# One attention and expert layer: projections moved ahead of the attention steps, the end reordered, and the first residual and normalisation handed to TensorE, GpSimd and ScalarE

## The chip, the cores and the metric

The program runs on one core of one Trainium2 chip. The metric is the device time of one execution in microseconds; the kernel before took 244.71 us (median of 3 runs, 243.72 to 245.84).

## What the reference computes

```python
x = L0_attn_x                                    # (8, 256, 128), 8 batches, 2048 tokens
Q, K, V = x @ Wq + bq, x @ Wk + bk, x @ Wv + bv  # 16 heads of 8
attended = softmax(Q K^T / sqrt(8)) V            # 256 x 256 scores per head and batch
x = layernorm(x + attended @ Wo + bo)            # no gain, no offset
shared = (silu(x @ sw1) * (x @ sw3)) @ sw2       # 256 hidden
s = sigmoid(x @ router_w.T)                      # 8 experts; the top two of s + router_bias are picked
gates = s_sel / (sum of the two s_sel + 1e-9)
routed = sum over experts e of gates_e * (gelu(x @ ew1[e]) @ ew2[e])   # 128 hidden each
x = layernorm(x + shared + routed)
```

All in float32.

## The kernel before

Tokens lie in 8 batches of 256 and, for the feed-forward part, in 4 groups of 512. The whole order is written by hand in `lay_out_slots` (L65 to L142): a list of slots, each with at most one maxima step `m`, one scores step `s`, steps of probabilities times V `pv`, and a list of jobs. Every engine walks the same list and does its part of each slot, in order; semaphores alone hold the engines together.

- The first 14 slots are the **prologue**: the first projections of batch 0, maxima steps 0 to 11, and jobs that project later tokens: `k`, `q`, `v` with a unit number (512 tokens each).
- The **attention slots** s = 0 to 63 follow, 8 per batch. In each, TensorE forms scores for two heads (L819, into the two `ring` banks) and, 12 steps ahead, the maxima products (L828, three `max_bank`s); VectorE reduces the maxima (L656); ScalarE takes the exponent (L554); TensorE multiplies by V (L845). A scores product reuses the ring bank of the slot before, so it waits for that slot's exponent.
- Jobs of the batch just finished sit in the next batch's slots: `norm` (slot 2 of 8), `attT` (3), `wo` (4: the product with Wo, then residual add L695 and statistics L699, L702 on VectorE), `y` (5: GpSimd makes 1/sqrt of the variance, L480, L481, and writes the normalised rows, L483), `yT` (slot 8, which is slot 0 of the batch after: transposed, ScalarE writes the high part L610, VectorE the low part L706), `router` (9). The float32 products with the feed-forward weights use such high and low parts (three passes, L799 to L801). `route...`, `rank`, `den` are the top-two selection, on GpSimd and VectorE; `combT` and `load gates` send the gates through DRAM so that they can be read back to all partitions.
- `shift` (slot 4) splits the maxima and sends them through ScalarE's DMA queue (L605) to the query stack.
- The **end** has 40 units: for each, TensorE forms the upward product (`unit`), ScalarE the nonlinearity (L627 tanh for shared units, L629 Gelu for experts), VectorE the gated product (L761, L764 or L769), and two slots later TensorE accumulates the downward product (`down`, L981). Units 0 to 7 are the shared ones, 8 to 39 the experts of groups 0 to 3. Inside the first units lie the jobs of batch 7; the last group's selection is on VectorE (L720 to L753). Each group ends with `accT`, `finT`, `rstd2`, `norm2` and a store.

## Time and profile before

| | |
|---|---|
| median of 3 runs | 244.71 us |
| profiled execution, its own time | 239.34 us |
| its span, first to last instruction | 237.5 us |
| mean granted TensorE clock | 0.955 of full speed |
| TensorE, VectorE, ScalarE, GpSimd busy | 211.6, 159.9, 135.9, 98.7 us |

The profiled execution is 5.4 us under the median. Times in views count from the first instruction of the span. A granted clock of 1.00 is 2.4 GHz and 0.50 is 1.2 GHz. A share of busy time mixes stages, so each stage is read in its own stretch.

### The profile page before, as it was taken

The page shows a single profiled execution, that of the slowest core. Times are in us where ns is not written, and L with a number is a line of the kernel's source. Part 1 is how long each engine was busy: PE and PEld are TensorE (multiplying, and loading weights), DVE is VectorE, ACT ScalarE, POOL GpSimd, SP SyncE. Part 2 cuts the span into 40 slices and gives each one's busy share as a digit, 9 for nine tenths or more (in the row PEclk, how much of TensorE's full clock was granted, in tenths as well). Part 3 has the DMA queues.
Part 4 walks back from the last instruction along what each step waited for, and adds up shares of the span by engine and source line. Part 5 has one row for each costly group of instructions (what it writes and reads, how often), then busy time and mean ns, then how long its engine had stood idle before and what let it go on. Part 6 is the DMA issues. An engine that isn't in the chain of part 4 may idle for free.

```text
span 237.5 us, 4492 instructions
## 1 busy us (share of the span) xinstructions
PE 211.6 (89%) x1538; PEld 120.8 (51%) x1538; DVE 159.9 (67%) x354; ACT 135.9 (57%) x278; POOL 98.7 (42%) x187
## 2 busy tenths in 40 slices
PE   7997999889899989999899999986788999999970
PEld 7754754354445555546454555653434555555530
DVE  6689686479579899989993223663594365565644
ACT  2996266678777878777778874221524333434330
POOL 8888950244247669573956084042000002020203
PEclk9998559999979999999999999999999999999996
DMA  5471770243134100018000630000000260731011
GB/s 164 133 203 44 187 287 10 59 105 97 46 88 107 49 6 4 8 30 330 6 3 7 217 142 0 3 0 4 0 0 3 91 266 0 265 132 44 3 34 55
DMA packets 10422, 19.19 MB, mean 81 GB/s; under 512 B 1952, under 2 KB 7008, under 8 KB 9760
## 3 DMA queue, kind: packets, MB, share of 16 engines
q1 hardware_dynamic: 8976, 17.06, 22.4%
q10 hardware_dynamic: 1040, 1.05, 1.3%
q0 software_dynamic: 384, 0.79, 1.2%
q8 instruction: 13, 0.21, 0.4%
q14 instruction: 9, 0.07, 0.1%
HBM read 12.80 MB, written 1.11 MB: 59 GB/s over the span
## 4 chain that ended last, share of the span: by engine, by line
PE 64%; DVE 17%; ACT 9%; issue 5%; POOL 2%; ACTq 1%; POOLq 0%; DVEq 0%
PE ring L819 14%; PE pv_bank L845 11%; PE max_bank L981 8%; DVE top L656 4%; ACT probs_mem L554 4%; PE max_bank L828 3%; PE sum_bank L981 3%; PE ring L799 3%; PE ring L801 3%; PE ring L800 3%; DVE hid L769 2%; PE pv_bank L853 2%; DVE stats L780 2%; PE sum_bank L900 2%; PE misc_bank L900 1%
## 5 line engine op out<-in xcount | busy, mean ns | idle before, releaser
L656 DVE TENSOR_REDUCE top<-max_bank 128x2 f32<-128x512 f32 x128 | 80.9, 681 | 12.8 <-PE max_bank L828 12.7
L554 ACT ACTIVATE probs_mem<-ring 128x512 f32<-128x512 f32 x128 | 70.2, 597 | 20.3 <-PE ring L819 18.7
L819 PE MATMUL ring<-qstack,kstack 32*128 32x256 f32 x256 | 46.0, 338 | 6.4 <-ACT probs_mem L554 4.2
L828 PE MATMUL max_bank<-kstack,qstack 32*128 32x256 f32 x256 | 45.7, 349 | 1.2 <-DVE top L656 0.9
L819 PEld LDWEIGHTS ring<-qstack,kstack 32*128 32x128 f32 x256 | 29.5, 192 | 26.5 <-ACT probs_mem L554 14.5
L845 PE MATMUL pv_bank<-probs_mem,v 128*18 128x256 f32 x512 | 41.4, 396 | 0.4 <-ACT probs_mem L554 0.4
L629 ACT ACTIVATE xt<-ring 128x512 f32<-128x512 f32 x32 | 19.1, 597 | 35.2 <-PE ring L801 35.2
L769 DVE TENSOR_TENSOR hid<-xt,gates_mem 128x512 f32<-128x512 f32 x32 | 21.9, 689 | 22.3 <-ACT xt L629 22.2
L981 PE MATMUL max_bank<-hid,wf 128*128 128x512 f32 x60 | 31.8, 612 | 2.1 <-DVE hid L769 1.5
L828 PEld LDWEIGHTS max_bank<-kstack,qstack 32*128 32x128 f32 x256 | 29.1, 198 | 6.0 <-DVE top L656 1.9
L799 PE MATMUL ring<-yt_hi,wf_lo 128*128 128x512 f32 x40 | 30.7, 767 | 0.0
L489 POOL TENSOR_SCALAR rstd<-mv 128x4 f32<-128x4 f32 (+1 forms) x5 | 2.2, 441 | 65.1 <-DVE mv L783 65.0
L470 POOL TENSOR_TENSOR gates_mem<-gates_mem 128x512 fp32r<-128x512 f32 x6 | 7.6, 1268 | 20.9 <-ACT gates_mem L595 20.9
L801 PE MATMUL ring<-yt_hi,wf_hi 128*128 128x512 f32 x40 | 15.8, 395 | 0.0
L800 PE MATMUL ring<-yt_lo,wf_hi 128*128 128x512 f32 x40 | 15.8, 395 | 0.0
L845 PEld LDWEIGHTS pv_bank<-probs_mem,v 128*18 128x18 f32 x512 | 8.7, 97 | 9.9 <-issue 1.0
L981 PEld LDWEIGHTS max_bank<-hid,wf 128*128 128x128 f32 x60 | 9.6, 188 | 8.0 <-DVE hid L769 6.2
L627 ACT ACTIVATE xt<-ring 128x512 f32<-128x512 f32 x8 | 4.8, 597 | 14.8 <-PE misc_bank L801 7.0
L483 POOL TENSOR_SCALAR xs<-res,mv,rstd 128x128 f32<-128x128 f32 x16 | 12.7, 801 | 0.9
L799 PEld LDWEIGHTS ring<-yt_hi,wf_lo 128*128 128x128 f32 x40 | 7.6, 190 | 9.3 <-issue 7.9
L800 PEld LDWEIGHTS ring<-yt_lo,wf_hi 128*128 128x128 f32 x40 | 7.6, 190 | 8.6 <-issue 8.6
L981 PE MATMUL sum_bank<-hid,wf 128*128 128x512 f32 x20 | 10.7, 619 | 1.3 <-DVE hid L769 1.1
(211 smaller groups left out, 320.8 us busy)
## 6 DMA issues: line engine op xcount, KB each, us to landing
gates_mem<-gate_scratch SPq DMA_DIRECT2D x4, 2048.0 KB, 7.7
kstack<-gates_mem SPq DMA_DIRECT2D x36, 64.0 KB, 2.1
qstack<-gates_mem SPq DMA_DIRECT2D x24, 64.0 KB, 2.1
wf<-w_ffn_dram SPq DMA_DIRECT2D x1, 1408.0 KB, 7.4
xs<-x_dram SPq DMA_DIRECT2D x4, 256.0 KB, 5.6
xt<-x_t_dram SPq DMA_DIRECT2D x3, 256.0 KB, 4.3
qstack<-gates_mem POOLq DMA_DIRECT2D x12, 64.0 KB, 2.6
out_dram<-xs SPq DMA_DIRECT2D x3, 256.0 KB, 2.3
```

The lines of the kernel that those rows point to most:

```text
L483: ins = pool.tensor_scalar(xs[:, QT * n + t, :], res1[:, t, :], mv1[:, t, 0:1], rstd1[:, t:t + 1], ALU.subtract, ALU.mult)
L554: nc.scalar.activation(probs[:, i % 2, s_heads(s)[r], :], ring_of(("scores", 2 * s + r))[:, :], ACT.Exp, scale=SCALE).then_inc(probs_made, 1)
L629: nc.scalar.activation(act_out[:, b % 2, :], bank[:, :], ACT.Gelu).then_inc(act_made, 1)
L656: dve.tensor_reduce(top[:, m_heads(m)[r], t, :], max_bank[(2 * m + r) % NMAX][:, :].rearrange("p (h k) -> p h k", h=2), AX.X, ALU.max).the ...
L769: dve.tensor_tensor(hid[:, b % NHB, :], act_out[:, b % 2, :], gates_mem[:, g % 2, e * GT:(e + 1) * GT], ALU.mult).then_inc(hid_dve, 1)
L799: mm(out_ap, w_lo, m_hi, start=first, stop=False)
L800: mm(out_ap, w_hi, m_lo, start=False, stop=False)
L801: return mm(out_ap, w_hi, m_hi, start=False, stop=last)
L819: ins = mm(ring_of(("scores", 2 * s + r))[:, kt * S:(kt + 1) * S], kstack[rows, t, k:k + P], qstack[rows, t, b * S:(b + 1) * S], start=Tru ...
L828: ins = mm(max_bank[(2 * m + r) % NMAX][:, qt * S:(qt + 1) * S], qstack[rows, t, q:q + P], kstack[rows, t, b * S:(b + 1) * S], start=True, ...
L845: ins = mm(pv_bank[32 * j:32 * j + 2 * VW, 0:S], v[:, (QT * b + kt) * H // 2 + HPS * n + j, k * VW:(k + 2) * VW], probs[:, p // 2 % 2, j, ...
L981: mm(acc_bank[g][:, :], wf[:, c:c + P], hid[:, b % NHB, :], start=n == 0, stop=n == NSH + NE - 1).then_inc(down_made, 1)
```

## The change

It has three parts.

1. Prologue: units 1 and 0 of V are projected earlier and units 2 of K and Q move from attention slots 6 and 8 into the prologue; unit 1 of V uses a ring bank. K, Q and V of unit 3 move from slots 16 to 21 to slots 8 to 13, V of unit 2 from slot 11 to 4. The stores of unit 2 stand in slot 0, ahead of the load of the feed-forward weights on SyncE.
2. End: the first eight units are the experts of group 0, the next eight the shared ones, then the experts of groups 1 to 3. The jobs of batch 7 stand further apart (`norm` 2, `attT` 4, `wo` and `y` 5, `yT` 10, `router` 12), `router` of batch 6 moves into the end, and the last group's selection runs on GpSimd and VectorE like that of the others. Before, each batch's `router` was one slot after `yT`; now three slots after. `hid` now shares the memory of `probs`.
3. First residual: TensorE adds x by a product with the identity (new L924), VectorE's statistics read PSUM, GpSimd makes 1/sqrt and the shift, ScalarE writes the normalised rows (new L636). ScalarE copies the transposed rows (new L642) and GpSimd makes both parts (new L508, L509).

```diff
@@ -69,8 +71,8 @@
         slots[n + 2].m = n
     for n, job in ((0, ("first", 0)), (0, ("first", 1)), (0, ("high", 0)), (1, ("first", 2)),
                    (2, ("first", 3)), (2, ("first", 4)), (3, ("first", 5)), (4, ("first", 6)), (5, ("first", 7)), (7, ("k", 1)),
-                   (8, ("store", (1, 1))), (9, ("q", 1)), (9, ("store", (1, 0))), (10, ("shift", 0)), (12, ("v", 0)),
-                   (12, ("split rw", 0))):
+                   (8, ("v", 1)), (8, ("store", (1, 1))), (9, ("q", 1)), (9, ("store", (1, 0))), (10, ("shift", 0)),
+                   (10, ("v", 0)), (11, ("k", 2)), (12, ("split rw", 0)), (13, ("q", 2))):
         slots[n].jobs.append(job)
     at, m = {}, 12
...
-    put(0, ("load w", 0))
+    put(0, ("store", (2, 1)), ("store", (2, 0)), ("load w", 0))
     put(1, ("bo", 0))
-    put(2, ("add bo", 0))
-    put(3, ("v", 1))
-    put(4, ("add bo", 1))
-    for s, unit in ((6, 2), (16, 3)):
-        put(s, ("k", unit))
-        put(s + 1, ("store", (unit, 1)))
-        put(s + 2, ("q", unit))
-        put(s + 4, ("store", (unit, 0)))
-        put(s + 5, ("v", unit))
-        put(s + 6, ("add bo", unit))
+    for n in range(NG):
+        put(2 + 2 * n, ("add bo", n))
+    put(4, ("v", 2))
+    for n, job in ((8, ("k", 3)), (9, ("store", (3, 1))), (10, ("q", 3)), (12, ("store", (3, 0))), (13, ("v", 3))):
+        put(n, job)
     for n in range(PIECES):
         put(18 + 2 * n, ("split w", n))
     for b in range(1, NB):
         slot = next(n for n in range(len(slots)) if slots[n].m == 8 * b + 7) + 1
         slots[slot].jobs.insert(0, ("shift", b))
+    route = (("route0", 1), ("sig", 2), ("route1", 3), ("route2", 4), ("route3", 6), ("rank", 8), ("route4", 9), ("den", 10),
+             ("route5", 11))
     for b in range(NB - 1):
         first = 8 * (b + 1)
-        for kind, n in (("norm", 2), ("attT", 3), ("wo", 4), ("y", 5), ("yT", 8), ("router", 9)):
+        for kind, n in (("norm", 2), ("attT", 3), ("wo", 4), ("y", 5), ("yT", 8)):
             put(first + n, (kind, b))
+        if b < NB - 2:
+            put(first + 11, ("router", b))
         if b % 2:
-            g = b // 2
-            for kind, n in (("route0", 10), ("sig", 11), ("route1", 12), ("route2", 13), ("route3", 15), ("rank", 17),
-                            ("route4", 18), ("den", 19), ("route5", 20)):
-                put(first + n, (kind, g))
-            put(first + 22, ("combT", b - 1))
-            put(first + 23, ("combT", b))
-            if g < 2:
-                put(first + 25, ("load gates", g))
-
-    unit_at = [NHALF + u + (u >= 6) for u in range(NUNITS)]
-    for u, s in enumerate(unit_at):
-        put(s, ("unit", u))
-        put(s + 2, ("down", u))
-    for kind, n in (("norm", 1), ("attT", 2), ("wo", 3), ("y", 3), ("yT", 6), ("router", 7), ("route a", 8), ("route b", 9),
-                    ("route c", 10)):
-        put(NHALF + n, (kind, NB // 2 - 1 if kind.startswith("route ") else NB - 1))
-    put(NHALF + 12, ("combT", NB - 2))
-    put(NHALF + 13, ("combT", NB - 1))
+            for kind, n in route:
+                put(first + 11 + n, (kind, b // 2))
+            if b // 2 < 2:
+                put(first + 24, ("combT", b - 1))
+                put(first + 25, ("combT", b))
+                put(first + 27, ("load gates", b // 2))
+    for u in range(NUNITS):
+        put(NHALF + u, ("unit", u))
+        put(NHALF + u + 2, ("down", u))
+    for n, job in ((2, ("norm", NB - 1)), (4, ("attT", NB - 1)), (5, ("wo", NB - 1)), (5, ("y", NB - 1)), (8, ("router", NB - 2)),
+                   (9, ("combT", 4)), (10, ("yT", NB - 1)), (10, ("combT", 5)), (12, ("router", NB - 1)), (12, ("load gates", 2)),
+                   (24, ("combT", NB - 2)), (25, ("combT", NB - 1)), (26, ("load gates", 3))):
+        put(NHALF + n, job)
+    for kind, n in route:
+        put(NHALF + 12 + n, (kind, NG - 1))
     for g in range(NG):
-        s = unit_at[NSHARED + NE * g + NE - 1]
-        if g < 2:
-            put(s + 2, ("load gates", g + 2))
+        s = NHALF + last_of(g)
...
+        latest, rotation = {}, 0
+
+        early_bank = {("v", 1): (ring[1], 6), ("v", 0): (pv_bank, 7)}
         for n, slot in enumerate(slots):
-            banks = [misc_bank, sum_bank] if n < tail else [misc_bank] + max_bank[1:] if n < tail + 3 else [misc_bank, pv_bank]
+            banks = ([misc_bank, sum_bank] if n < tail else [misc_bank, max_bank[2]] if n < tail + 3
+                     else [misc_bank, pv_bank, max_bank[2]] if n < tail + 14 else [misc_bank, pv_bank])
             for kind, u in slot.jobs:
...
                     if kind == "y":
                         pool.wait_ge(stats_made, n + 1)
                         chain(pool.tensor_scalar(rstd1[:, :], mv1[:, :, 1], EPS, None, ALU.add))
+                        pool.tensor_scalar(shift1[:, :], mv1[:, :, 0], -1.0, None, ALU.mult)
                         chain(pool.tensor_tensor(rstd1[:, :], rstd1[:, :], minus_half[:, 0:QT], ALU.pow))
-                        for t in range(QT):
-                            ins = pool.tensor_scalar(xs[:, QT * n + t, :], res1[:, t, :], mv1[:, t, 0:1],
-                                                     rstd1[:, t:t + 1], ALU.subtract, ALU.mult)
-                        ins.then_inc(y_made, 1)
+                        pool.tensor_tensor(shift1[:, :], shift1[:, :], rstd1[:, :], ALU.mult).then_inc(rstd_made, 1)
+                    if kind == "yT":
+                        wait_taken(pool, (kind, n))
+                        c = slice(n * S, (n + 1) * S)
+                        chain(pool.tensor_scalar(yt_hi[:, c], yt_raw[:, n % 2, :], 1.0, None, ALU.mult))
+                        pool.tensor_tensor(yt_lo[:, c], yt_raw[:, n % 2, :], yt_hi[:, c].bitcast(F32), ALU.subtract).then_inc(yt_made, 1)
...
                     if kind == "attT":
                         nc.scalar.copy(att_t[:, :], misc[:, 0:S]).then_inc(misc_act, 1)
+                    if kind == "y":
+                        act.wait_ge(rstd_made, b + 1)
+                        for t in range(QT):
+                            ins = nc.scalar.activation(xs[:, QT * b + t, :], misc_of(("wo", b))[:, t * P:(t + 1) * P], ACT.Identity,
+                                                       bias=shift1[:, t:t + 1], scale=rstd1[:, t:t + 1])
+                        ins.then_inc(y_made, 1)
                     if kind == "yT":
-                        nc.scalar.copy(yt_hi[:, b * S:(b + 1) * S], misc[:, 0:S]).then_inc(yt_hi_made, 1)
+                        if b >= 2:
+                            act.wait_ge(yt_made, b - 1)
+                        nc.scalar.copy(yt_raw[:, b % 2, :], misc[:, 0:S]).then_inc(misc_act, 1)
...
                     if kind == "wo":
                         dve.wait_ge(misc_made, made[kind, b])
-                        dve.wait_ge(xb_made, b // 2 + 1)
                         if b:
                             dve.wait_ge(y_made, b)
-                        dve.tensor_tensor(res1[:, :, :], misc[:, 0:S].rearrange("p (t d) -> p t d", t=QT),
-                                          xs[:, QT * b:QT * b + QT, :], ALU.add).then_inc(misc_dve, 1)
-                        wait_taken(dve, (kind, b))
                         for t in range(QT):
-                            ins = dve.bn_stats(stats1[:, t, :], res1[:, t, :])
+                            ins = dve.bn_stats(stats1[:, t, :], misc[:, t * P:(t + 1) * P])
                         chain(ins)
...
                     if kind == "wo":
                         wait_taken(pe, ("attT", b))
+                        pe.wait_ge(xb_made, b // 2 + 1)
                         for t in range(QT):
-                            ins = mm(misc[:, t * P:(t + 1) * P], att_t[:, t * P:(t + 1) * P], wa[:, 3, :],
-                                     start=True, stop=True)
+                            mm(misc[:, t * P:(t + 1) * P], att_t[:, t * P:(t + 1) * P], wa[:, 3, :], start=True, stop=False)
+                            ins = mm(misc[:, t * P:(t + 1) * P], ident[:, :], xs[:, QT * b + t, :], start=False, stop=True)
                         ins.then_inc(misc_made, 1)
```

How instructions move. First, TensorE in the prologue, from the first `k` job to the first scores product (L900 and new L892: Q or K projection; L903 and new L895: V projection, except that the new L903 is the shift's transpose, which was L911). Before:

```order
L900 MATMUL misc_bank<-xt,wa 128x512
L828 MATMUL max_bank<-kstack,qstack 128x256 x8
L900 MATMUL sum_bank<-xt,wa 128x512
L828 MATMUL max_bank<-kstack,qstack 128x256 x4
L911 MATMUL misc_bank<-ident,top_parts 32x128 x2
L828 MATMUL max_bank<-kstack,qstack 128x256 x8
L903 MATMUL sum_bank<-wa,xt 128x128 x4
L828 MATMUL max_bank<-kstack,qstack 128x256 x4
L819 MATMUL ring<-qstack,kstack 128x256
```

Now:

```order
L892 MATMUL misc_bank<-xt,wa 128x512
L819 MATMUL max_bank<-kstack,qstack 128x256 x4
L895 MATMUL ring<-wa,xt 128x128 x4
L819 MATMUL max_bank<-kstack,qstack 128x256 x4
L892 MATMUL sum_bank<-xt,wa 128x512
L819 MATMUL max_bank<-kstack,qstack 128x256 x4
L903 MATMUL misc_bank<-ident,top_parts 32x128 x2
L895 MATMUL pv_bank<-wa,xt 128x128 x4
L819 MATMUL max_bank<-kstack,qstack 128x256 x4
L892 MATMUL sum_bank<-xt,wa 128x512
L819 MATMUL max_bank<-kstack,qstack 128x256 x8
L892 MATMUL misc_bank<-xt,wa 128x512
```

Three projections stand there that were not: V of unit 1, K of unit 2 and, last before the scores, Q of unit 2.

Second, ScalarE from slot 3 to slot 8 of a batch in the middle (`probs_mem` is the exponent, `xs` the normalised rows). Before:

```order
L608 COPY att_t<-misc_bank 128x256
L554 ACTIVATE probs_mem<-ring 128x512 x2
L602 CAST top_rows<-sum_bank 32x256
L605 DMA qstack<-top_rows 8x4x256
L554 ACTIVATE probs_mem<-ring 128x512 x2
L562 COPY att_raw<-pv_bank 128x256
L554 ACTIVATE probs_mem<-ring 128x512 x6
L610 CAST yt_hi<-sum_bank 128x256
```

Now:

```order
L632 COPY att_t<-misc_bank 128x256
L578 ACTIVATE probs_mem<-ring 128x512 x2
L626 CAST top_rows<-sum_bank 32x256
L629 DMA qstack<-top_rows 8x4x256
L578 ACTIVATE probs_mem<-ring 128x512 x2
L586 COPY att_raw<-pv_bank 128x256
L636 ACTIVATE xs<-misc_bank,shift,rstd 128x128 x2
L578 ACTIVATE probs_mem<-ring 128x512 x6
L642 COPY yt_raw<-sum_bank 128x256
```

The two new activations stand between the exponents of slot 5 and those of slot 6, and wait for GpSimd.

Third, ScalarE at the start of the end (L661 Gelu, L659 tanh, L646 the router's exponent). Before there was one table load, at unit 8:

```order
L614 ACTIVATE expl<-pv_bank 128x16
L627 ACTIVATE xt<-ring 128x512
L629 ACT_TABLE_LOAD
L629 ACTIVATE xt<-ring 128x512 x4
L620 COPY comb_t<-pv_bank 8x256
```

Now:

```order
L661 ACT_TABLE_LOAD
L661 ACTIVATE xt<-ring 128x512
L586 COPY att_raw<-pv_bank 128x256
L661 ACTIVATE xt<-ring 128x512 x4
L632 COPY att_t<-max_bank 128x256
L661 ACTIVATE xt<-ring 128x512
L636 ACTIVATE xs<-misc_bank,shift,rstd 128x128 x2
L661 ACTIVATE xt<-ring 128x512 x2
L659 ACTIVATE xt<-ring 128x512
L646 ACT_TABLE_LOAD
L646 ACTIVATE expl<-max_bank 128x16
L659 ACTIVATE xt<-ring 128x512
```

A third load follows at unit 16. The normalised rows of batch 7 stand between the Gelus of units 5 and 6.

## Rows read from the trace of the kernel before

**Rows 1.** Busy time by stretch: span, PE, PEld, DVE, ACT, POOL (count), clock, DMA.
```profile
84.00:126.00 42.00, 39.67 (x460) 22.02 (x454) 38.95 (x90) 32.98 (x71) 28.61 (x69) 1.00 0.14 55
```

**Rows 2.** Same view for the exponents (L554): busy, count, clock, by batch, half batch.
```profile
28.30:44.65 16.35, 8.91 (x16) 0.79 0.39 130
44.65:59.50 14.85, 8.72 (x16) 1.00 0.40 100
59.50:77.05 17.55, 8.70 (x16) 0.90 0.32 81
77.05:90.25 13.20, 8.81 (x16) 1.00 0.10 26
...
28.30:36.90 8.60, 4.56 (x8) 0.59 0.69 232
36.90:44.65 7.75, 4.36 (x8) 1.00 0.06 16
```

**Rows 3.** Busy time of one microsecond of the prologue, columns as in rows 1.
```profile
21.00:22.00 1.00, 0.26 (x4) 0.06 (x2) 0.93 (x3) 1.00 (x2) 0.79 (x1) 0.82 0.44 113
```

**Rows 4.** Timeline of the prologue: start, length, engine, line, [idle before, its releaser].
```profile
19.70 1.13 PE L900 MATMUL sum_bank<-xt,wa 128*128 128x512 f32 x2
25.01 2.08 PE L903 MATMUL sum_bank<-wa,xt 128*128 128x128 f32 x8
28.33 0.60 ACT L554 ACTIVATE probs_mem<-ring 128x512 f32<-128x512 f32 x1 [0.60 <-PE ring L819]
```

**Rows 5.** Timeline of ScalarE around K of unit 2 in attention slot 6.
```profile
40.22 1.10 ACT L554 ACTIVATE probs_mem<-ring 128x512 f32<-128x512 f32 x2
42.27 0.69 ACT L591 ACTIVATE gates_mem<-sum_bank,wa 128x512 fp32r<-128x512 f32 x1 [0.95 <-PE sum_bank L900]
43.42 1.08 ACT L554 ACTIVATE probs_mem<-ring 128x512 f32<-128x512 f32 x2
```

**Rows 6.** Timeline around one batch's Wo product, by engine.
```profile
111.91 0.61 PE L930 MATMUL misc_bank<-wa,att_t 128*128 128x128 f32 x4
115.79 0.38 PE L819 MATMUL ring<-qstack,kstack 32*128 32x256 f32 x1
...
112.86 0.41 DVE L695 TENSOR_TENSOR res<-misc_bank,xs 128x256 f32<-128x256 f32 x1
113.83 0.25 DVE L702 BATCH_NORM_AGGREGATE mv<-stats 128x2 f32<-128x6 f32 x2
...
115.11 0.22 POOL L480 TENSOR_SCALAR rstd<-mv 128x2 f32<-128x2 f32 x1
116.25 1.59 POOL L483 TENSOR_SCALAR xs<-res,mv,rstd 128x128 f32<-128x128 f32 x2
...
114.44 0.61 ACT L554 ACTIVATE probs_mem<-ring 128x512 f32<-128x512 f32 x1
```

**Rows 7.** One source line, ns of one: activations with bias and scale from memory.
```profile
L582 ACT ACTIVATE probs_mem<-ring,first_cols x8: 556/568/587, 6.4 to 15.2; 128x256 fp32r<-128x256 f32 x8
```

**Rows 8.** Timeline of the end: last exponents, table load, downward products and a stall.
```profile
142.44 1.08 ACT L554 ACTIVATE probs_mem<-ring 128x512 f32<-128x512 f32 x2 [0.38 <-PE ring L819]
...
170.22 1.28 ACT L629 ACT_TABLE_LOAD   x1
...
154.68 1.02 PE L981 MATMUL max_bank<-hid,wf 128*128 128x512 f32 x2
...
157.34 1.02 PE L981 MATMUL max_bank<-hid,wf 128*128 128x512 f32 x2
...
162.42 0.38 PE L952 MATMUL pv_bank<-ident,comb 128*8 128x128 f32 x2 [2.67 <-POOL comb L530]
...
228.94 1.12 PE L981 MATMUL max_bank<-hid,wf 128*128 128x512 f32 x2 [0.44 <-DVE hid L769]
```

**Rows 9.** The chain that ended last: downward products, eight units apart.
```profile
210.37 1.12 PE max_bank L981 x2
...
224.13 1.12 PE max_bank L981 x2
```

More of the change, by code:

```diff
@@ L38 @@
 NSHARED = NG * NSH
+SHARED = range(NE, NE + NSHARED)
 NUNITS = NG * (NSH + NE)
@@ L146, in group_of, with first_of, last_of @@
 def group_of(u):
-    return divmod(u, NSH) if u < NSHARED else ((u - NSHARED) // NE, NSH + (u - NSHARED) % NE)
+    if u in SHARED:
+        return divmod(u - SHARED.start, NSH)
+    e = u if u < NE else u - NSHARED
+    return e // NE, NSH + e % NE
+def first_of(g):
+    return min(u for u in range(NUNITS) if group_of(u)[0] == g)
+def last_of(g):
+    return max(u for u in range(NUNITS) if group_of(u)[0] == g)
 FIN = [(g, 0, TPG) for g in range(NG - 1)] + [(NG - 1, t, t + TPG // 2) for t in (0, TPG // 2)]
@@ L325, in wait_taken @@
                 wait_hid(eng, u[1])
+            elif taker(u) == "y":
+                eng.wait_ge(y_made, u[1] + 1)
             else:
@@ L329, in wait_bank @@
         def wait_bank(eng, u):
-            if before[u] is not None:
+            if u in early_bank:
+                eng.wait_ge(first_read, early_bank[u][1])
+            elif before[u] is not None:
                 wait_taken(eng, before[u])
@@ L563, in _ @@
                 for kind, b in slot.jobs:
-                    if TAKER.get(kind) == "act" or kind == "yT":
+                    if TAKER.get(kind) == "act":
                         act.wait_ge(misc_made, made[kind, b])
@@ L730, in _ @@
-                    if kind == "route b":
-                        chain(dve.tensor_scalar(tie[:, :, :, :], diff[:, :, :, :], 0.0, None, ALU.is_equal))
-                        chain(dve.tensor_scalar(diff[:, :, :, :], diff[:, :, :, :], 0.0, None, ALU.is_gt))
-                        for t in range(TPG):
-                            ins = dve.tensor_tensor(tie[:, t, :, :], tie[:, t, :, :], earlier[:, :, :], ALU.mult)
-                        chain(ins)
-                        chain(dve.tensor_tensor(diff[:, :, :, :], diff[:, :, :, :], tie[:, :, :, :], ALU.add))
-                        dve.tensor_reduce(rank[:, :, :], diff[:, :, :, :], AX.X, ALU.add).then_inc(route_dve, 1)
@@ L809, in wait_ring @@
                     pe.wait_ge(probs_made, n + 1)
-                elif n < NSHARED:
-                    pe.wait_ge(sh_read, n + 1)
+                elif n in SHARED:
+                    pe.wait_ge(sh_read, n - SHARED.start + 1)
                 else:
```

80 lines of the change are left out of this document (27 added, 53 removed).

## The prediction

> **What bounds the kernel now.** I read the stages first, because no engine is the limit throughout. In the middle of attention two engines are nearly full: of 42 us TensorE is busy 39.67 and VectorE 38.95, ScalarE 32.98 [rows 1]. The exponents mark the batches: 13.20 us for an undisturbed one, 16.35 for the first and 17.55 for the third [rows 2]. The first is long because the granted clock is 0.50 (1.2 GHz) for most of its first half: 8.60 us against 7.75 for the second half, although that one carries a K projection [rows 2]. The clock fell in the microsecond in which TensorE had only 0.26 us of work [rows 3]. A K or Q projection inside attention lengthens its slot to 43.42 - 40.22 = 3.20 us, since ScalarE takes its two copies before the next exponents [rows 5]; the next slot, up to 44.65 [rows 2], takes 1.23, so one costs 1.95. The third batch has two of them. The end lasts from the last exponent, 143.52, to the last downward product, 230.06: 86.5 us [rows 8]. In its dense part eight units take 13.76 us [rows 9]; its first part has stalls, the longest 2.67 us, where TensorE waits for GpSimd's gates [rows 8].
>
> **A, the prologue.** V of unit 1, K and Q of unit 2 are added ahead of the first scores. At full clock each is 1.1 us of TensorE (1.13 for a Q projection) [rows 4], 3.3 in all. The first fills the hole in which the clock fell, and V of unit 0, 2.08 us at half clock [rows 4], should then take half. I expect the clock to hold and the extra work to be nearly absorbed; but Q of unit 2 stands last, and its two copies by ScalarE (0.69 each [rows 5]) come before the first exponent. That one moves from 28.33 to about 29.4: +1.1. First batch: two halves like the second, without its K: 2 x (7.75 - 1.95) = 11.6, plus 0.6 for V of unit 2 and 0.4 for the Wo bias, an estimate: 12.6, rounded up to 12.8 since its jobs differ, against 16.35: -3.5. Second: loses one projection, gains two: +1.95. Third: becomes like the fourth, 13.20 for 17.55: -4.35. Sum **A = -4.8**. If the clock falls as before, the two added projections cost 2.1 us each, the first exponent comes 4.6 later, the first batch gains 2.4 instead of 3.5 and A is -0.2. On SyncE the 24 stores of unit 2 now precede the weight load. They are due at maxima step 32, in attention slot 20, and the weights in slot 18, both over 20 us later; I cost them at nothing, and were they late, TensorE's maxima of slot 20 would wait.
>
> **B, the first residual.** VectorE loses the add of 0.41 [rows 6] and the low part, about as long since it too reads 256 columns of PSUM. TensorE gains two products of the kind of the Wo ones, whose four records take 0.61 with their overlap [rows 6]; I take 0.45 for the two. GpSimd trades two 0.8 us operations [rows 6] for three or four small ones and the two parts, which nothing needs for three slots. Statistics read from PSUM have no row; from no change up to 0.2 more each, since the add that reads twice the columns from there takes 0.41. I take no change, because reading PSUM has not made that add slow.
> What decides is the new wait on ScalarE. Take the batch of [rows 6]. The aggregate ends at 114.08; without the add at 113.65. GpSimd takes 1.14 from L480 to L483, and two more small operations of 0.22 with gaps add 0.5: 115.4, if GpSimd is free. ScalarE then writes two tiles: an activation with both operands from memory is 0.57 us for 256 columns [rows 7], so 0.45 to 0.57 for 128; I take 0.9 for both: 116.3. Only then comes the exponent of slot 6, 0.61: 116.9 instead of 115.05. The scores of slot 7 reuse its bank and started at 115.79 [rows 6]; they start 1.1 later. Behind them wait the maxima and VectorE. About 0.3 comes back, since VectorE has caught up by then and the router's product fills a wait three slots later: **0.8 per batch** for five batches, 4.0. For batch 0 V of unit 3 lies in the same slot and covers the wait: 0.1. Batch 7's slots have no maxima to hide behind: 0.45 for the product and 0.85 for the wait, together 1.3. **B = +5.4.** Bounds per batch: -0.4 (the add's time passes through, the wait is covered) and +1.9.
>
> **C, the end.** Walked with the prices of the rows, from the last exponent: first downward product after transposing, 1.28 for the table load [rows 8], 0.60 Gelu and 0.69 product: 4.0. Six more experts with three jobs of batch 7: 11.3. Then unit 6's Gelu waits behind the same chain as in B, and its downward product is 2.1 late. Eight shared units, 157.34 - 154.68 = 2.66 each less a wait of 0.28 there [rows 8], with two router products, four transposes and a finish among them: 22.4. Remaining 24 units at 1.62 with two finishes and the last steps: 42.9 (13.76 for eight with a finish [rows 9]). Sum 82.7 against 86.5: **C = -3.9** with rounding. The 2.67 stall and VectorE's selection between the first experts are gone. The second table load has about 2 us of cover from TensorE's work on unit 9, the third about as much as it takes.
> Each load is 1.28 us here, followed at once by its activation [rows 8]. The Trainium skill (ScalarE: Activation LUTs, What ACT_TABLE_LOAD costs) gives 2.66 us for a switch with a drain, and its section on table sets asks to group activations by set. That speaks against two more loads. The trace shows no drain.
>
> **Sum.** -4.8 + 5.4 - 3.9 = -3.3 on 239.34: 236.0 for a profiled execution. That execution is 5.4 under the median of the runs; the difference applied to 244.71 gives **241.4**. What a measurement can tell from no change is 1%, 2.4 us: under 242.3 is faster, over 247.2 slower.
>
> **The rivals.**
> - Forecast, 0.43: 241.4, own range 238.5 to 245. For it: every step stands in a queue order.
> - The clock falls in the prologue all the same, 0.20. VectorE's reductions pace the prologue, so TensorE keeps holes. A = -0.2, total +1.3: 246.0.
> - VectorE's relief passes through and the wait on ScalarE is covered, 0.17. For it: VectorE is busy 38.95 of 42 us [rows 1] and loses 0.8 per batch. Against: the exponent of slot 6 is behind the wait. B = 7 x -0.4 = -2.8, total -11.5: 233.2.
> - Slower, 0.12: GpSimd is late. In the shown batch the aggregate was ready at 114.08 and L480 began at 115.11, because the selection's operations were ahead of it in GpSimd's queue [rows 6]. Now ScalarE, and behind it TensorE, would wait for that. It decides from 1.6 us per batch on; at +1.0 more for seven batches the total is -3.3 + 7.0 = +3.7: 248.4. Against: the selection now starts a slot after `y`.
> - Switches cost more than their load, 0.08. A drain of half a load to a whole one behind the first and the third would sit on the path: at 1.3 each nearly +2.5, 243.9. The Trainium skill's 2.66 us (ScalarE: Activation LUTs, What ACT_TABLE_LOAD costs) is this rival's size.
>
> The first and last are on the faster or the same side by their spread (0.43 gives 0.27 faster, 0.15 same), the second same or slower. **Faster 0.50, same 0.31, slower 0.19.** Range 233.5 to 248.5: from just above the third case's value, half of which lies below, to the fourth's; it leaves out about 0.1 below and 0.08 above.
>
> **What would show it.** Clock: no 0.50 before the first exponent, which starts near 29.4; batches of 12.7, 16.8 and 13.5 us. B: ScalarE idle before L636 until GpSimd's L504, 0.7 us or more in most batches; batch periods in the middle 0.8 above 13.3, and VectorE well under its 93%. C: 82 to 84 us from last exponent to last downward product, first one about 4 us in, a stall of about 2 us at unit 6. The prediction fails if the clock drops in another place, if the ScalarE wait is under 0.3 us, or if GpSimd starts L501 late.

## The result, and the profile after

The changed kernel takes 254.94 us (median of 6 runs, 251.58 to 262.17), the kernel before 244.42 beside it (240.35 to 246.08): ratio 1.0427, 95% interval 1.0236 to 1.0618. 241.4 was forecast, with 233.5 to 248.5 as the range. It is slower by 4.3%. The ratio leaves out runs more than 1.5% above the fastest of their kernel (it compares 251.58, 252.26 and 253.26 with 240.35 and 243.72), and since single runs of one kernel lie up to 5.5% apart, the main differences below are given on the medians and between the fastest runs.

The profiled execution took 251.58 us, its span is 249.8, against 239.34 and 237.5. Its page:

```profile
span 249.8 us, 4579 instructions
PE 222.4 (89%) x1570; PEld 127.5 (51%) x1570; DVE 153.5 (61%) x317; ACT 143.6 (58%) x296; POOL 110.7 (44%) x224
PEclk9999956999995699979999798699999999999997
```

The third line is the granted clock in 40 slices. Before, it had one deep dip, at 22 to 35 us, and a shallow one. Now there are five: 5 and 6 from 31 us on, 5 and 6 from 75 on, 7 at 106, 7 at 137, and 8 and 6 from 150 on (a slice is 6.2 us). The batches, as in [rows 2] by the exponents' line (span, busy ScalarE, clock):

```profile
30.15:45.60 15.45, 8.80 (x16) 0.67 0.48 130
45.60:62.70 17.10, 8.68 (x16) 1.00 0.54 168
62.70:78.25 15.55, 8.80 (x16) 0.91 0.08 22
78.25:95.20 16.95, 8.68 (x16) 0.78 0.01 3
95.20:109.75 14.55, 8.69 (x16) 0.99 0.01 3
109.75:125.70 15.95, 8.66 (x16) 0.90 0.35 136
125.70:140.30 14.60, 8.69 (x17) 1.00 0.01 3
140.30:156.00 15.70, 8.68 (x16) 0.83 0.35 136
```

Every batch from the fourth on is longer than the 13.20 of [rows 2]. The two at the full clock take 14.55 and 14.60; the others, where the clock fell, 15.7 to 16.95. Three engines are less busy than in [rows 1], although the stretch is longer (44 us for 42):

```profile
95.20:139.20 44.00, 40.15 (x436) 22.06 (x436) 32.45 (x73) 32.78 (x73) 27.44 (x71) 0.96 0.13 52
```

VectorE fell from 38.95 of 42 us to 32.45 of 44, so its relief came, and bought nothing. The timeline around one batch's normalisation shows where the time sits. The columns are those of [rows 6]:

```profile
134.96 1.08 ACT L578 ACTIVATE probs_mem<-ring 128x512 f32<-128x512 f32 x2 [0.91 <-PE ring L810]
135.00 0.25 DVE L730 BATCH_NORM_AGGREGATE mv<-stats 128x2 f32<-128x6 f32 x2
135.34 0.24 POOL L501 TENSOR_SCALAR rstd<-mv 128x2 f32<-128x2 f32 x1 [1.65 <-DVE mv L730]
136.66 0.19 POOL L504 TENSOR_TENSOR shift<-shift,rstd 128x2 f32<-128x2 f32 x1
136.89 0.81 ACT L636 ACTIVATE xs<-misc_bank,shift,rstd 128x128 f32<-128x128 f32 x2 [0.58 <-POOL shift L504]
137.59 1.08 ACT L578 ACTIVATE probs_mem<-ring 128x512 f32<-128x512 f32 x2
138.23 0.98 PE L810 MATMUL ring<-qstack,kstack 32*128 32x256 f32 x4 [1.08 <-ACT probs_mem L578]
138.83 1.08 ACT L578 ACTIVATE probs_mem<-ring 128x512 f32<-128x512 f32 x2 [0.16 <-PE ring L810]
```

ScalarE waits 0.58 us for GpSimd's last small operation (L504), writes the rows (0.81), and only then comes the exponent of slot 6, at 137.59. Behind it TensorE stood still for 1.08 us. Such a hole, 1.05 to 1.08 long, lies in six batches: it ends at 75.20, 93.15, 107.69, 123.68, 138.23 and 153.94. The clock in the stretches after some of them, and after the longest hole of all, which lies behind the first exponents:

```profile
28.90:30.80 1.90, 0.53 (x9) 0.31 (x8) 1.55 (x3) 1.78 (x4) 1.90 (x5) 1.00 0.75 219
31.00:32.00 1.00, 1.00 (x8) 0.62 (x8) 0.53 (x1) 0.82 (x2) 0.98 (x3) 0.55 0.72 207
75.00:86.00 11.00, 10.80 (x86) 4.93 (x86) 6.58 (x11) 6.30 (x14) 3.69 (x8) 0.53 0.01 1
109.00:113.00 4.00, 4.00 (x40) 1.99 (x36) 2.02 (x4) 2.35 (x6) 1.35 (x4) 0.57 0.01 2
140.00:144.00 4.00, 4.00 (x29) 1.69 (x28) 0.00 (x0) 2.58 (x6) 1.01 (x2) 0.57 0.02 6
154.00:161.00 7.00, 7.00 (x36) 3.56 (x37) 0.70 (x1) 4.08 (x7) 4.34 (x7) 0.51 0.00 1
```

The clock is 0.50 (1.2 GHz) from just after the holes that end at 30.80 and 75.20, from about 2 us after those of 107.69 and 138.23, and from at once after that of 153.94. After those of 93.15 and 123.68 it stayed at 1.00. A hole is thus no certain fall, but every fall up to here follows one (e1 and e11 will show falls that follow none). The two profiled executions, before and after, laid side by side:

| | forecast | measured |
|---|---|---|
| first exponent, 28.33 to 30.18 | +1.1 | +1.85 |
| batches 0 to 2, 48.76 to 48.10 | -5.0 | -0.66 |
| batches 3 to 6, 53.82 to 62.02 | +3.2 | +8.20 |
| batch 7, 12.61 to 15.61 | +1.3 | +3.00 |
| last exponent to last downward product, 86.54 to 86.38 | -3.9 | -0.16 |
| sum | -3.3 | +12.2 |

The forecast column is A, B and C put where they act. Only the second batch came out as forecast (17.10 for 16.8 + 0.1).

### The profile page after: what moved, and what is told of

Read it like the earlier page. It is cut to its first block and busy times, and to the rows that moved or that the text cites. A ratio compares the mean times of both kernels' runs of the same rounds, so it can differ in the third digit from the quotient of the medians.

```text
span 249.8 us, 4579 instructions
## 1 busy us (share of the span) xinstructions
PE 222.4 (89%) x1570; PEld 127.5 (51%) x1570; DVE 153.5 (61%) x317; ACT 143.6 (58%) x296; POOL 110.7 (44%) x224
## 3 DMA queue, kind: packets, MB, share of 16 engines
q10 hardware_dynamic: 1040, 1.05, 1.3%
## 5 line engine op out<-in xcount | busy, mean ns | idle before, releaser
L810 PE MATMUL ring<-qstack,kstack 32*128 32x256 f32 x256 | 49.2, 360 | 10.9 <-ACT probs_mem L578 9.3
L810 PEld LDWEIGHTS ring<-qstack,kstack 32*128 32x128 f32 x256 | 31.1, 206 | 37.5 <-ACT probs_mem L578 26.9
L819 PE MATMUL max_bank<-kstack,qstack 32*128 32x256 f32 x256 | 47.0, 355 | 1.1 <-DVE top L688 0.8
L836 PE MATMUL pv_bank<-probs_mem,v 128*18 128x256 f32 x512 | 45.7, 436 | 0.0
L760 DVE TENSOR_TENSOR probs_mem<-xt,gates_mem 128x512 f32<-128x512 f32 x32 | 22.4, 703 | 34.7 <-ACT xt L661 34.7
L661 ACT ACTIVATE xt<-ring 128x512 f32<-128x512 f32 x32 | 19.0, 597 | 30.3 <-PE ring L792 29.3
L971 PE MATMUL max_bank<-probs_mem,wf 128*128 128x512 f32 x60 | 32.0, 614 | 1.8 <-DVE probs_mem L760 1.4
L790 PE MATMUL ring<-yt_hi,wf_lo 128*128 128x512 f32 x40 | 31.9, 797 | 0.0
L508 POOL TENSOR_SCALAR yt_hi<-yt_raw 128x256 fp32r<-128x256 f32 x8 | 6.8, 856 | 28.2 <-ACT yt_raw L642 28.1
L659 ACT ACTIVATE xt<-ring 128x512 f32<-128x512 f32 x8 | 4.8, 597 | 15.5 <-PE misc_bank L792 5.6
L971 PEld LDWEIGHTS max_bank<-probs_mem,wf 128*128 128x128 f32 x60 | 9.7, 188 | 7.8 <-DVE probs_mem L760 5.8
L491 POOL TENSOR_TENSOR gates_mem<-gates_mem 128x512 fp32r<-128x512 f32 x6 | 7.6, 1270 | 13.2 <-ACT gates_mem L619 13.2
L971 PE MATMUL sum_bank<-probs_mem,wf 128*128 128x512 f32 x20 | 10.4, 602 | 1.7 <-DVE probs_mem L760 1.7
```

Source lines behind the costliest of these rows:

```text
L491: pool.tensor_tensor(part[:, i, 1, :], qk[:, i, :], part[:, i, 0, :].bitcast(F32), ALU.subtract).then_inc(qk_lo_made, 1)
L661: nc.scalar.activation(act_out[:, b % 2, :], bank[:, :], ACT.Gelu).then_inc(act_made, 1)
L760: dve.tensor_tensor(hid[:, b % NHB, :], act_out[:, b % 2, :], gates_mem[:, g % 2, e * GT:(e + 1) * GT], ALU.mult).then_inc(hid_dve, 1)
L790: mm(out_ap, w_lo, m_hi, start=first, stop=False)
L810: ins = mm(ring_of(("scores", 2 * s + r))[:, kt * S:(kt + 1) * S], kstack[rows, t, k:k + P], qstack[rows, t, b * S:(b + 1) * S], start=Tru ...
L819: ins = mm(max_bank[(2 * m + r) % NMAX][:, qt * S:(qt + 1) * S], qstack[rows, t, q:q + P], kstack[rows, t, b * S:(b + 1) * S], start=True, ...
```

## The experiments

Two theories, with the second in two forms, stood at first. WAIT: the wait of ScalarE leaves TensorE idle for about 1 us in each batch, and the clock falls behind these holes. ORDER or LOAD: it is the moved work itself that costs, and the hole only shows where there was slack. Beside each run stood runs of the kernel before, with a median of 245.15 us for e1 to e4, 246.22 for e5 to e8 and 246.01 for e9 to e12; its fastest runs took 239.19, 240.31 and 239.21, its slowest 252 in all three. The changed kernel ran with the result and again in e9, so the differences to it from e1 to e8 are across sessions.

### e1: without the residual part

```diff
-        TAKER = {..., "wo": "y", "yT": "act", ...}
+        TAKER = {..., "wo": "dve", "yT": "dve", ...}
...
-                            ins = mm(misc[:, t * P:(t + 1) * P], ident[:, :], xs[:, QT * b + t, :], start=False, stop=True)
...
+                        dve.tensor_tensor(res1[:, :, :], misc[:, 0:S].rearrange("p (t d) -> p t d", t=QT),
+                                          xs[:, QT * b:QT * b + QT, :], ALU.add).then_inc(misc_dve, 1)
```

> The changed kernel with its first residual and normalisation as before (VectorE adds, GpSimd writes the rows, VectorE makes the low part); prologue and end as changed, the router three slots after the transpose. Changed kernel: 254.9 median, before 244.4. Theory WAIT (ScalarE's wait for GpSimd leaves TensorE idle for about 1 us in every batch, and the granted clock falls behind such holes): batches 3 to 7 fall from 15.4 to about 13.5 us, the 2.6 us stall at unit 7 goes and the clock is 1.00 from there on: 240 to 242. Theory ORDER (the changed prologue, the moved routers and the order of the end cost it): stays at 250 or more.

Measured: 241.5 us (241.3 to 247.3, 4 runs). The time is as WAIT has it; 13.4 us come back with this part (10.3 between the fastest runs). ORDER falls with it; WAIT and LOAD part only in e3, e4 and e8, because e1 takes away the load together with the wait. One part of what WAIT expected did not come: the clock was not held in batch 7, which took 20.0 us. It fell at 128 us, with no hole like those above before it:

```profile
128.00:152.00 24.00, 23.73 (x139) 11.12 (x137) 3.03 (x10) 12.95 (x27) 8.76 (x22) 0.50 0.23 89
```

### e2: without the end part

```diff
-    for u in range(NUNITS):
-        put(NHALF + u, ("unit", u))
-        put(NHALF + u + 2, ("down", u))
+    unit_at = [NHALF + u + (u >= 6) for u in range(NUNITS)]
+    for u, s in enumerate(unit_at):
+        put(s, ("unit", u))
+        put(s + 2, ("down", u))
```

> The kernel before with the prologue part and the residual part, the end in the order of before (the router three slots after the transpose, since GpSimd now makes its parts). WAIT: nearly as slow as the changed kernel, 252 to 257, with the same holes at L636's successor and the same falls of the clock. ORDER (the end's order is the cost): back to 245 or less.

Measured: 263.5 us (260.8 to 265.3, 4 runs), slower still than either theory had it. From the last exponent to the last downward product it takes 91.1 us for the 86.4 of the changed kernel. The end's order is not the cost. It helps the residual part: in the old order ScalarE waits 3.75 us for GpSimd before it writes the rows of batch 7 (3.02 in the changed kernel), and the units behind wait for those.

### e3: the y job one slot later

```diff
-        for kind, n in (("norm", 2), ("attT", 3), ("wo", 4), ("y", 5), ("yT", 8)):
+        for kind, n in (("norm", 2), ("attT", 3), ("wo", 4), ("y", 6), ("yT", 8)):
...
-    for n, job in (..., (5, ("wo", NB - 1)), (5, ("y", NB - 1)), ...
+    for n, job in (..., (5, ("wo", NB - 1)), (6, ("y", NB - 1)), ...
```

> The changed kernel with the y job one slot later (slot 6 instead of 5, in the end too), so that ScalarE comes to the two activations after the exponents of slot 6. WAIT: ScalarE hardly waits, each batch is 0.9 us shorter and the clock falls no more in batches 2 to 7; 242 to 246. LOAD (TensorE's two identity products and the router's new place make the slots longer, the wait is only where the slack is shown): no more than 2 us gained, 252 or more.

Measured: 260.8 us (259.1 to 268.6, 4 runs). My expectation failed, and the trace says why. GpSimd's queue and ScalarE's in one batch:

```profile
102.22 0.23 POOL L545 TENSOR_SCALAR den_ok<-den 128x4 f32<-128x4 f32 x1 [2.41 <-DVE den_inv L742]
103.72 0.25 POOL L554 TENSOR_TENSOR comb<-picked,mask 128x32 f32<-128x32 f32 x1
104.06 0.22 POOL L501 TENSOR_SCALAR rstd<-mv 128x2 f32<-128x2 f32 x1
105.58 0.81 ACT L636 ACTIVATE xs<-misc_bank,shift,rstd 128x128 f32<-128x128 f32 x2 [3.08 <-POOL shift L504]
```

In this batch GpSimd's four small operations now stand behind `route5`, whose first operation itself waits 2.41 us for VectorE; in others they stand behind another part of the selection. ScalarE's wait grew from 0.58 to 3.08 us here; in batches 3 to 6 it is 2.45, 3.08, 2.44 and 1.89. This speaks against LOAD too: TensorE's work is the same, only a wait is longer, and 5.9 us are lost on the median of the changed kernel (7.5 between the fastest runs). In the end alone the later slot helped: 84.3 us for 86.4, without the stall at unit 6.

### e4: the holes filled

```diff
+                if s is not None and s % 8 == 6 and s > 16:
...
+                    wait_taken(pe, last)
+                    for _ in range(5):
+                        mm(bank_of[last][:, 0:P], ident[:, :], ident[:, :], start=True, stop=True)
```

> The changed kernel with five products of identity by identity (128x128, results never read) in slot 6 of batches 2 to 7, just where TensorE waits for the exponent behind L636. They remove no wait. If holes in TensorE's work are what the clock falls behind: the clock stays 1.00 in batches 2 to 7 and about 5 of the 10.5 us come back, 249 to 251. If the falls are not tied to the holes: the clock falls as before and the time is 255 or more.

Measured: 244.7 us (243.9 to 245.7, 4 runs): 10.2 us less than the changed kernel (7.7 between the fastest runs), with more work and the same wait. That is more than the 5 expected. In its trace the wait stands as it did, the hole is filled (L876), and from batch 1 to the end of attention the clock is 1.00:

```profile
131.98 0.81 ACT L636 ACTIVATE xs<-misc_bank,shift,rstd 128x128 f32<-128x128 f32 x2 [0.58 <-POOL shift L504]
132.18 1.38 PE L876 MATMUL sum_bank<-ident 128*128 128x128 f32 x10
44.40:149.90 105.50, 101.42 (x1082) 58.93 (x1082) 70.21 (x154) 79.61 (x174) 51.69 (x124) 1.00 0.21 74
```

The same stretch of the changed kernel:

```profile
45.60:156.00 110.40, 101.06 (x1026) 54.33 (x1029) 70.33 (x154) 80.19 (x174) 51.66 (x124) 0.91 0.20 70
```

These falls of the clock are caused by the holes. They cost 4.9 us here (110.40 - 105.50), and more in other executions, as the medians say; e9 shows one.

### e5, e6, e7: each part alone on the kernel before

```diff
-    put(0, ("load w", 0))
+    put(0, ("store", (2, 1)), ("store", (2, 0)), ("load w", 0))
...
+                   (10, ("v", 0)), (11, ("k", 2)), (12, ("split rw", 0)), (13, ("q", 2))):
```

> The kernel before with the prologue part alone. The prediction's term A: -4.8, 240 against 244.4, with the clock held; with the fall that the changed kernel shows behind the first exponents, WAIT and ORDER alike expect first exponent +1.0 to +1.8, batches 0 to 2 at 44 to 45 us for 48.8, in all 241 to 243, and no fall of the clock in batches 1 to 7.

Measured: 238.1 us (237.4 to 238.8, 4 runs).

```profile
30.05:73.50 43.45, 26.20 (x48) 0.92 0.41 120
73.50:127.50 54.00, 35.12 (x65) 1.00 0.12 44
```

This is under the 240 of term A and the 241 to 243 of the theories (between the fastest runs, -2.9). First exponent +1.75, batches 0 to 2 at 43.5 us for 48.8, batches 3 to 7 as before. The end takes 88.0 us for 86.5; the clock fell there too, at 159 us, just as a stall of 2.67 us ended. In this trace it also fell once in the prologue, at 19 us, long before the first exponent (columns as in [rows 1]), and so it did in e4:

```profile
18.00:23.00 5.00, 5.00 (x21) 3.07 (x21) 3.34 (x6) 3.14 (x8) 3.81 (x5) 0.66 0.16 39
```

```diff
+SHARED = range(NE, NE + NSHARED)
...
-    for kind, n in (("norm", 1), ("attT", 2), ("wo", 3), ("y", 3), ("yT", 6), ("router", 7), ("route a", 8), ("route b", 9),
+    for n, job in ((2, ("norm", NB - 1)), (4, ("attT", NB - 1)), (5, ("wo", NB - 1)), (5, ("y", NB - 1)), (8, ("router", NB - 2)),
```

> The kernel before with the end part alone (experts of group 0 first, two more table loads, selection of the last group on GpSimd, routers three slots after the transpose). The prediction's term C without its wait at unit 6: last exponent to last downward product 80.6 for 86.5, 238.5 to 240 in all. Rival SWITCHES (table loads cost more than their load, or the moved selection stalls TensorE again): 84 us or more there and 242 to 246 in all.

Measured: 246.5 us (239.2 to 249.1, 4 runs): unclear as a time, since the spread is larger than the effect (fastest runs 239.2 and 240.3). In its profiled execution (239.2) the end takes 82.4 us for 86.5, from the last exponent's end at 147.20 to 229.58. That lies between the 80.6 of term C and the 84 of the rival:

```profile
146.11 1.09 ACT L576 ACTIVATE probs_mem<-ring 128x512 f32<-128x512 f32 x2 [0.38 <-PE ring L808]
228.46 1.12 PE L967 MATMUL max_bank<-probs_mem,wf 128*128 128x512 f32 x2 [0.43 <-DVE probs_mem L758]
28.40:78.90 50.50, 26.44 (x48) 0.86 0.35 97
```

What it gains there is lost in the attention: in batches 0 to 2, at 50.5 us for 48.8, where the clock stayed low longer (to 39 us, not 35) and fell again at 42, and in batches 3 to 7, at 68.3 us for 66.4, for a reason that no run here isolates.

```diff
+                            ins = mm(misc[:, t * P:(t + 1) * P], ident[:, :], xs[:, QT * b + t, :], start=False, stop=True)
...
+                    if kind == "y":
+                        act.wait_ge(rstd_made, b + 1)
...
-        hid = sb("hid", [P, NHB, GT])
+        hid = probs_mem[:, 0:NHB * GT].rearrange("p (n t) -> p n t", n=NHB)
```

> The kernel before with the residual part alone (and the routers three slots after the transpose, which GpSimd's parts need; hid in the memory of probs). WAIT: each batch from 3 on 1.2 to 1.5 us longer at full clock, holes of about 1 us behind L636's successor, and the clock falls behind some of them in batches 2 to 7: 254 to 262. LOAD or the prediction's term B: +5.4, 250 at most, and no new falls of the clock.

Measured: 269.0 us (267.2 to 271.4, 4 runs), +22.7 (+26.9 between the fastest runs), four times the term B and more than WAIT had. The end alone is 9.6 us longer there (96.1), with the wait of e2 and a clock of 0.51 to 0.57 in three stretches of it.

### e8: ScalarE's two activations alone one slot later

```diff
-        for kind, n in (("norm", 2), ("attT", 3), ("wo", 4), ("y", 5), ("yT", 8)):
+        for kind, n in (("norm", 2), ("attT", 3), ("wo", 4), ("y", 5), ("y act", 6), ("yT", 8)):
...
-                    if kind == "y":
+                    if kind == "y act":
                         act.wait_ge(rstd_made, b + 1)
```

> The changed kernel with ScalarE's two activations alone one slot later (after the exponents of slot 6); GpSimd's four small operations stay in slot 5, ahead of the selection. WAIT: ScalarE no longer waits for L504, 0.7 us per batch come back and TensorE's hole shrinks from about 1.1 to 0.5 us, so that most falls of the clock go too: 244 to 249. If it is ScalarE's added work and not the wait that makes the hole: the hole moves to slot 7, and the time stays at 252 or more.

In the end the two activations stay where they were. Measured: 237.0 us (236.4 to 240.3, 4 runs): 17.9 us less than the changed kernel (15.2 between the fastest runs), and better than expected. With it the change as a whole is faster than the kernel before: 9.2 us on the medians, 3.9 between the fastest runs (236.42 and 240.31). GpSimd's chain is unchanged, and ScalarE no longer waits for it in attention:

```profile
86.15 1.10 ACT L578 ACTIVATE probs_mem<-ring 128x512 f32<-128x512 f32 x2
87.12 0.81 ACT L636 ACTIVATE xs<-misc_bank,shift,rstd 128x128 f32<-128x128 f32 x2
87.81 1.10 ACT L578 ACTIVATE probs_mem<-ring 128x512 f32<-128x512 f32 x2
```

From the exponents of one slot to those of the next it takes 1.66 us with the rows between them, where it took 2.63 (134.96 to 137.59) in the changed kernel. Batches 2 to 4 are 13.60, 13.60 and 13.70 us:

```profile
61.85:75.45 13.60, 8.72 (x16) 1.00 0.11 28
75.45:89.05 13.60, 8.73 (x16) 1.00 0.01 4
89.05:102.75 13.70, 8.73 (x16) 1.00 0.02 5
```

One hole of another kind was left in it, and the clock fell 1.6 us after it (119 to 122):

```profile
117.36 0.38 PE L810 MATMUL ring<-qstack,kstack 32*128 32x256 f32 x1 [1.60 <-DMA qstack<-top_rows]
119.00:123.00 4.00, 4.00 (x36) 1.83 (x36) 2.80 (x5) 2.85 (x7) 3.58 (x8) 0.57 0.01 4
```

### e9: the changed kernel again

> The changed kernel once more, beside the others on one chip. 252 to 258 if the first measurement stands.

Measured: 257.7 us (253.3 to 260.6, 4 runs). Its batches 1 to 7 took 116.1 us at a mean clock of 0.85, where the first trace has 110.4 at 0.91:

```profile
44.80:160.90 116.10, 106.64 (x1022) 56.69 (x1022) 70.17 (x153) 80.78 (x174) 51.80 (x124) 0.85 0.19 66
```

The program and its six holes (1.05 to 1.09 us) are the same. What differs is after how many of them the clock falls, five here and four in the first trace, and how long it stays low: a mean clock of 0.85 over 116.10 us is about 35 us at 0.50, one of 0.91 over 110.40 about 20. Against the 105.50 us of e4 these cost 10.6 and 4.9, an estimate of a quarter to a third of a microsecond for each one at half clock. In these two traces the difference in time lies there.

### e10: the residual part alone, ScalarE's activations one slot later

The edit of e8 on the kernel of e7.

> The residual part alone on the kernel before (269.0), with ScalarE's two activations one slot later in the attention; in the end they stay where they were. WAIT: the attention gets at least 10 us shorter than in e7, since the holes and the falls of the clock in it go, 252 to 259 with the end's own stalls left. If the slot matters only beside the other two parts: 265 or more.

Measured: 248.6 us (247.3 to 252.0, 4 runs), 20.3 less than e7 and under the 252 to 259 expected. The slot decides without the other parts too. In the profiled execution (252.0) batches 3 to 6 are down to 57.2 us from 69.0 in e7, and the end still takes 92.5 us for the 86.5 of the kernel before, with the wait of e2.

### e11 and e12: the two stalls that were left

e8, with the last group's gates one slot later (e11); and that, with the hole behind the first exponents filled (e12):

```diff
-                   (24, ("combT", NB - 2)), (25, ("combT", NB - 1)), (26, ("load gates", 3))):
+                   (25, ("combT", NB - 2)), (26, ("combT", NB - 1)), (27, ("load gates", 3))):
...
+                if s == 0:
+                    wait_taken(pe, ("v", 0))
+                    for _ in range(5):
+                        mm(pv_bank[:, 0:P], ident[:, :], ident[:, :], start=True, stop=True)
```

> e8 (ScalarE's rows one slot later) with the two transposes of the last group's gates and their load one slot later too (25, 26 and 27 of the end for 24, 25 and 26). TensorE waits 1.61 us there for GpSimd's L554: that goes, 1.0 to 1.6 less than e8 (ratio to before 0.963): ratio 0.957. Rival: the gates of the last group come late for unit 32, and a wait of the same size stands there.

Measured for e11: 240.0 us (235.1 to 244.1, 4 runs): unclear. Two of the four runs are at 235.1 and 236.2, the others at 244; in the profiled one the clock fell at 129.5 us, for 17 us in batch 7, although TensorE had had no hole over 0.3 us in the 14 us before. The wait at the gates is gone; the end takes 84.6 us for e8's 85.5.

> e11 with five products of identity by identity in attention slot 0, where TensorE waits 1.4 us for the first exponent behind the two copies of the last projection (results never read). If the clock's fall at 30 to 31 us hangs on that hole: no 0.50 between 30 and 41 us, batch 0 at 12.0 to 13 us for 15.4, ratio to before 0.945 to 0.95. If it does not: the same as e11.

Measured for e12: 235.1 us (233.6 to 241.0, 6 runs), the fastest of all, 10.9 under the median of the kernel before beside it, which is a ratio of 0.956 where 0.945 to 0.95 was expected; between the fastest runs it is 5.6 (233.60 and 239.21). The clock is 1.00 from the first exponent to the end of the attention. The view begins inside the ten records of the five products, which start at 29.21:

```profile
29.76 0.83 PE L874 MATMUL pv_bank<-ident 128*128 128x128 f32 x6
30.00:43.20 13.20, 11.60 (x128) 6.92 (x128) 11.56 (x20) 9.76 (x21) 9.31 (x11) 1.00 0.47 128
43.20:141.40 98.20, 93.95 (x1022) 51.66 (x1022) 69.72 (x153) 78.25 (x174) 50.57 (x123) 1.00 0.24 80
```

Batch 0 takes 13.2 us for 15.45, a little more than the 12.0 to 13 expected. TensorE no longer waits at the last group's gates, and the end takes 83.8 us. Part of this is chance: no late transfer (e8) fell into this execution, and the clock stayed at 1.00 after two holes of the size of those above (1.17 us, up to 37.24, and 1.06, up to 145.65).

## Why the prediction was wrong

**The step that failed** is the last one of B, "0.8 per batch". It priced the wait of ScalarE as a shift of the exponents, and left TensorE's clock out of it. The prediction had read in [rows 3] that the clock fell where TensorE had a hole, and used that for the prologue alone. It worked out itself that the scores of slot 7 would start 1.1 us later, which is the hole of 1.05 to 1.08 us that the trace shows in six batches, and did not ask what the clock would do behind it. Its list of what could go wrong names "the clock drops in another place"; no rival had it, so the range was too narrow above.

The profiled execution was forecast 3.3 us shorter than that of the kernel before and is 12.2 longer, so 15.5 have to be explained. By the traces about 8 of them are the clock, at which no term of the forecast put anything: 2.3 in batch 0 (15.46 us; 13.16 in e12, where it did not fall), 4.9 in batches 1 to 7 (e4) and 0.9 before the first downward product. About 3.4 are the wait at full clock, mis-sized at 0.8 per batch; 2.8 the rest of the end, where the walk of C left out a unit; 1.1 the later first exponent and batch 0 itself. So the clock fails B, and A too by "I expect the clock to hold"; C fails by its sum.

By the runs, of the 17.9 us between the changed kernel and e8, 10.2 is what comes back when the holes are filled and the wait stays (e4), and 7.7 is the rest, the wait itself; between the fastest runs the shares are 7.7 and 7.5 of 15.2. The traces agree on the second: at full clock batches 1 to 7 take 105.5 us in e4 and 98.2 in e12. The three medians come from three sessions, in which the kernel before had 244.4, 245.2 and 246.2.

- **Clock behind the wait.** Forecast: none. Shown by e4, which leaves the wait and only fills the holes. The Trainium skill (TensorE: Matmul & The Clock Gate, A second HAM failure mode: psum-queue depth-cycling) says that a TensorE which stands still for a moment between groups of products often enough can swing between the two levels of its clock. The traces of the changed kernel agree, and show it already with holes of about 1.05 us that lie a whole batch apart.
- **Size of the wait at full clock.** Forecast 0.8 per batch. Batches 3 to 6 of e4 take 59.3 us and those of e12, whose ScalarE does not wait, 54.6: 1.2 per batch. The sign and the chain (aggregate, four small operations, two activations, exponent, scores) were right; GpSimd's four took 1.5 us (135.34 to 136.85), where 1.6 was forecast, and the rows 0.81 for 0.9. The 0.3 that was to come back did not.
- **The rest of B.** Batches 3 to 6 take 54.6 us in e12 and 54.0 in e5, which has no residual part: 0.15 per batch. So what is left of the residual part, once the wait is gone, costs next to nothing, and gains nothing: the third rival, by which VectorE's relief is worth 0.4 per batch, is refuted. That VectorE was busy 93% of the time did not make it the bound.
- **GpSimd late**, the fourth rival, did not happen in the changed kernel (L501 begins 0.1 us after the aggregate ends), but it is real: e3 made it happen by one slot, with waits of 1.9 to 3.1 us in batches 3 to 6 where 0.55 had stood.
- **A, the prologue.** Forecast -4.8. Alone it gives -8.1 on the medians, -2.9 between the fastest runs beside each other (237.4 and 240.3), and in the profiled executions -3.4 up to the last exponent (140.1 for 143.5). The first exponent comes 1.8 us later and not 1.1, and the clock was not held. In the changed kernel it fell at 31 us, behind the hole of 1.4 us that Q of unit 2 itself makes, where TensorE waits for the first exponent and this for the copies. The prediction gave a fall 0.20, before the exponent. In this trace it came just after; in those of e4 and e5 it came at both places (19 and 33 us), so that the second rival is in part true. With the hole filled, batch 0 takes 13.2 (e12), for 12.8 forecast.
- **C, the end.** Forecast 82.7 us with a stall at unit 6. Alone 82.4, without that stall, for the 80.6 that this makes; in the changed kernel 86.4. The walk counts 1 + 6 + 8 + 24 = 39 units, and there are 40: group 0 has seven experts after its first. The step left out, from unit 6 to unit 7, took 2.95 us (173.87 to 176.82), and the same in e6. First downward product: 5.2 us for 4.0, at 0.50 up to 160.8; in e8 4.3. The eight shared units, from the downward product at 176.82 to that at 198.17, took 21.4 for 22.4. The stall of the y chain came as forecast:

```profile
171.78 0.81 ACT L636 ACTIVATE xs<-misc_bank,shift,rstd 128x128 f32<-128x128 f32 x2 [3.02 <-POOL shift L504]
173.87 1.12 PE L971 MATMUL sum_bank<-probs_mem,wf 128*128 128x512 f32 x2 [1.73 <-DVE probs_mem L760]
```

  The walk of C had said that the 2.67 us stall at GpSimd's gates [rows 8] was gone. It was not; it is smaller, and stands where the last group's gates are transposed:

```profile
213.37 0.38 PE L942 MATMUL misc_bank<-ident,comb 128*8 128x128 f32 x2 [1.61 <-POOL comb L554]
```

- **Table loads.** The two more loads took 1.28 us each, as in [rows 8], and their activations follow at once:

```profile
177.05 1.28 ACT L646 ACT_TABLE_LOAD   x1
178.34 0.18 ACT L646 ACTIVATE expl<-max_bank 128x16 f32<-128x16 f32 x1
196.69 1.28 ACT L661 ACT_TABLE_LOAD   x1
197.98 0.60 ACT L661 ACTIVATE xt<-ring 128x512 f32<-128x512 f32 x1
```

  The rival of the dearer switch is refuted. The Trainium skill (ScalarE: Activation LUTs, What ACT_TABLE_LOAD costs) gives 2.66 us for a switch, of which 1.28 are the load and 1.38 a drain. The trace agrees on the load, 1.28; no drain shows beside it, and there the measurement decides.

Open: why the clock stayed at 1.00 after two of the six holes, and why its low stretches last 3 us after one hole and 10 after another. In e1 it fell at 128 us, where the last hole over 0.3 us was 0.46 us long and ended 3 us earlier, and stayed low for 24 us; in e11 it fell at 129.5 with no such hole in the 14 us before. The maxima have run out there in both. So holes of 1 us are one cause of falls, by e4 and e12, and not the only one; no run here isolates the other.

## What to carry to other kernels

When a change puts a wait into an in-order engine that feeds TensorE, price TensorE's hole twice: its length, and the stretch at half clock that may follow, for which the trace of before can have an example, as that of this kernel had in the prologue. Then look whether the consumer can stand one step later while the producer stays where it is: here that was worth 17.9 us on the medians, and moving both cost 5.9. Time the parts of a change apart, since one part's loss can hide the gains of the others, as here.

## What the runs showed of the hardware

- Six holes of about 1.05 us in 80 us of otherwise nearly full work were followed by four falls of TensorE's clock from 1.00 to 0.50 in one execution and by five in another (e9), each within about 2 us of its hole; with the holes filled by products whose results nobody reads, there was none (e4).
- A hole of this size is neither enough nor needed: the clock stayed at 1.00 after holes of 1.17 and 1.06 us in e12, and fell in e1 and e11 with none over 0.5 us in the 14 us before.
- Two executions of one program differ in how long the clock stays low (110.4 and 116.1 us for the same seven batches), and so does the time.
- Two batch statistics of 128 columns took 0.49 us read from PSUM (L727), the same as the pair read from SBUF in the kernel before.
